# Attention over a gathered half of the tokens: the start in another order, and a batch's mean, its product and its tail rows moved into its own batch

## The reference, cut to what matters

```python
xt = jnp.transpose(x, (0, 2, 1))
q = xt @ Wq.T
qh = q.reshape(B, T, NH, dk).transpose(0, 2, 1, 3)
scores = scale * jnp.einsum('bhqd,bhkd->bhqk', qh, qh)
logits = (scores * cmask + (1.0 - cmask) * NEG) * rmask
attn = jax.nn.softmax(logits, axis=-1)
ctx = jnp.einsum('bhqk,bhkd->bhqd', attn, qh)
out = ctx.transpose(0, 2, 1, 3).reshape(B, T, D) @ Wo.T
return x + jnp.transpose(out, (0, 2, 1))
```

## Time and profile before

| what | value |
|---|---|
| median of 3 runs | 1621.71 us (1619.72 to 1621.74) |
| the profiled execution, its own time | 1617.55 us |
| its span, first to last instruction | 1615.8 us |
| granted TensorE clock, mean | 0.981 |
| busy: TensorE | 1537.4 us (95%) |
| busy: GpSimd | 1339.1 us (83%) |
| busy: VectorE | 1185.3 us (73%) |
| busy: ScalarE | 854.3 us (53%) |

### The profile page before, as it was taken

How to read it: one execution, slowest core, us unless ns; L and a number is a source line. 1 busy time by engine, 2 the same in 40 slices (tenths; PEclk the granted TensorE clock), 3 DMA queues, 4 the chain that set the end, 5 groups by cost and what they waited for, 6 DMA issues and landing times. The chain is left out here.

```text
span 1615.8 us, 33177 instructions
## 1 busy us (share of the span) xinstructions
PE 1537.4 (95%) x10956; PEld 1222.4 (76%) x10956; DVE 1185.3 (73%) x2659; ACT 854.3 (53%) x2055; POOL 1339.1 (83%) x1069
## 2 busy tenths in 40 slices
PE   6798999999999999999999999999999999999995
PEld 3666777787877788787777777777877777777863
DVE  5356787877778787787878778787877778787773
ACT  2145556565555556555555655555555565555450
POOL 5558989898898989889898988989898898987771
PEclk9689999999999999999999999999999999999997
DMA  3434455454544545353554535445554544453410
GB/s 115 107 85 96 105 129 122 110 130 99 129 103 123 122 110 136 93 135 97 123 122 114 136 93 132 100 120 122 123 128 98 129 106 119 115 131 90 109 50 30
DMA packets 93810, 179.09 MB, mean 111 GB/s; under 512 B 24704, under 2 KB 24832, under 8 KB 93632
## 3 DMA queue, kind: packets, MB, share of 16 engines
q1 hardware_dynamic: 64448, 109.71, 30.0%
q0 software_dynamic: 29184, 67.17, 14.9%
HBM read 36.77 MB, written 33.55 MB: 44 GB/s over the span
## 5 line engine op out<-in xcount | busy, mean ns | idle before, releaser
L870 DVE TENSOR_REDUCE small_mxp<-max_scores 108x1 f32<-108x270 f32 x1280 | 546.7, 435 | 269.9 <-PE max_scores L1069 245.4
L751 ACT ACTIVATE small_Pt<-scores,small_kbias 108x270 f32<-108x270 f32 x1280 | 551.5, 483 | 343.9 <-PE scores L1088 335.9
L596 POOL TENSOR_TENSOR small_Pacc<-small_Pacc,small_Pt 108x540 f32<-108x540 f32 x384 | 517.8, 1349 | 117.1 <-ACT small_Pt L751 110.3
L1069 PE MATMUL max_scores<-small_ops 128*108 128x270 f32 x1280 | 412.0, 329 | 17.3 <-DVE small_mxp L870 16.3
L1100 PE MATMUL ctx_psum<-small_Pt,small_V 108*64 108x270 f32 x2560 | 313.1, 391 | 0.0
L900 DVE RECIPROCAL small_rsum<-small_rsum 128x67 f32<-128x67 f32 (+1 forms) x512 | 240.8, 532 | 77.6 <-ACT small_rsum L698 75.8
L1069 PEld LDWEIGHTS max_scores<-small_ops 128*108 128x108 f32 x1280 | 218.9, 173 | 86.3 <-issue 41.0
L1085 PE MATMUL scores<-small_ops 128*108 128x270 f32 x1280 | 270.8, 290 | 4.7 <-ACT small_Pt L751 4.5
L1100 PEld LDWEIGHTS ctx_psum<-small_Pt,small_V 108*64 108x64 f32 x2560 | 184.3, 137 | 106.9 <-issue 0.2
L1088 PE MATMUL scores<-small_ops 128*108 128x270 f32 x1280 | 263.6, 287 | 0.0
L1085 PEld LDWEIGHTS scores<-small_ops 128*108 128x108 f32 x1280 | 191.5, 173 | 25.5 <-ACT small_Pt L751 8.8
(11 more groups left out here) (108 smaller groups left out, 2366.2 us busy)
## 6 DMA issues: line engine op xcount, KB each, us to landing
small_ops<-small_H SPq DMA_DIRECT2D x512, 135.0 KB, 2.8
small_ops<-small_L SPq DMA_DIRECT2D x256, 135.0 KB, 2.7
small_ops<-small_mrow SPq DMA_DIRECT2D x128, 2.1 KB
small_xg<-x_rows,small_idx POOLq DMA_INDIRECT x80, 3.9
small_xtail<-x_rows,small_idx POOLq DMA_INDIRECT x80, 4.9
out_rows<-small_xtail,small_idx POOLq DMA_INDIRECT x80, 3.8
out_rows<-small_xg,small_idx POOLq DMA_INDIRECT x80, 3.8
wq_sb<-wq SPq DMA_DIRECT2D x1, 1024.0 KB, 5.3
```

Source lines behind the costliest of these rows:

```text
L596: nc.gpsimd.tensor_tensor(acc, other, t["Pt"][:R, p0], ALU.add).then_inc(pacc_step, 1)
L751: nc.scalar.activation(t["Pt"][:R, (NT * s + k) % f.NP, half, :], ST[(2 * (NT * h + k) + half) % 3][:R, 0:H], ACT.Exp, bias=t["kbias"][:R, ...
L870: nc.vector.tensor_reduce(t["mxp"][:R, h % 2, m // 2, m % 2:m % 2 + 1], MX[m % 2][:R, 0:H], AX.X, ALU.max).then_inc(mx_red, 1)
L1069: nc.tensor.matmul(MX[m % 2][:R, 0:H], ops[:, OPA, tile_cols(m // 2)], ops[:, OPB, half_cols(m % 2)], start=True, stop=True).then_inc(mx_r ...
```

## The change

It does four things, for the forms that are split (the one that runs here among them).

1. **Front, tables.** Batch 0's one-hots are made alone; those of all batches (`hot_tiles`) after the last xT, and the eight `hot_rows` in pairs behind the first four projections. TensorE makes the other 15 orders, unrolled and with fixed columns, two behind each row-maximum product of head 0 from the third on.
2. **Front, weights.** The transposed Wq is loaded first. GpSimd clears the operands before the gathers, gathers only five tiles of batch 0, and makes one low part. The high and low parts of Wo are made in quarters inside batch 0. G's four blocks are made ahead of the transposes, among them, and (two) among head 1's row-maximum products. VectorE no longer sums.
3. **Loop.** `sum_tokens`, `xbar` and `w` of a batch are made in the batch itself, for the last one too; `w` has one buffer. `xbar` moves from (6, 2) to (5, 2), `w` from (7, 3) and (7, 4) to (5, 3) and (5, 4); pair 5's projections, pair 4's values and pair 6's first projection move later.
4. **Loop, GpSimd.** The tail is gathered in head 0, and its rows are finished and scattered in heads 6 and 7; the 34 jobs are dealt out anew.

The buffers of the one-hot tables and of Wo's parts lie elsewhere in memory. The core of the diff:

```diff
-    ((4, 3), (4, 3), "proj", (4, 0)), ((4, 4), (4, 4), "proj", (4, 1)), ((5, 3), (5, 4), "proj", (5, 0)),
-    ((6, 0), (6, 1), "proj", (5, 1)), ((7, 0), (7, 1), "proj", (6, 0)), ((7, 3), (7, 4), "w", 0)]
-V_STEPS = {1: ((0, 2, 1), (0, 3, 0)), 2: ((4, 0, 0), (4, 0, 1)), 3: ((5, 0, 0), (5, 1, 0)), 4: ((6, 3, 0), (6, 4, 0))}
+    ((4, 3), (4, 3), "proj", (4, 0)), ((4, 4), (4, 4), "proj", (4, 1)), ((5, 3), (5, 4), "w", 0),
+    ((6, 0), (6, 1), "proj", (5, 0)), ((6, 3), (6, 4), "proj", (5, 1)), ((7, 3), (7, 3), "proj", (6, 0))]
+V_STEPS = {1: ((0, 2, 1), (0, 3, 0)), 2: ((4, 0, 0), (4, 0, 1)), 3: ((5, 0, 0), (5, 1, 0)), 4: ((7, 0, 0), (7, 1, 0))}
-XBAR_STEP = (6, 2, 1)
+XBAR_STEP = (5, 2, 1)
-ADD_W_AT = [(0, 0), (0, 1), (0, 3), (0, 4), (1, 0)]
-SCATTER_TAIL_AT = [(1, 1), (1, 3), (1, 4), (2, 0), (2, 1)]
-GATHER_TAIL_AT = [(2, 3), (2, 4), (3, 0), (3, 1), (3, 3)]
-SCATTER_AT = [(3, 4), (4, 0), (4, 1), (5, 0), (5, 1)]
-TAIL_SUM_AT = [(4, 3), (4, 4), (5, 2), (5, 3), (5, 4)]
-GATHER_AT = [(6, 0), (6, 1), (6, 3), (6, 4), (7, 0)]
-SUM_AT = [(7, 1), (7, 2), (7, 3), (7, 4)]
-FIRST_SUM_AT = [(2, 1), (2, 2), (3, 1), (3, 2)]
+WO_HIGH_AT = [(0, 3), (0, 4), (1, 0), (1, 1)]
+WO_LOW_AT = [(1, 3), (1, 4), (2, 0), (2, 1)]
+GATHER_TAIL_AT = [(0, 1), (0, 2), (0, 3), (0, 4), (1, 0)]
+SUM_AT = [(0, 0), (1, 1), (1, 2), (1, 3), (1, 4), (2, 0), (3, 0), (3, 2), (4, 0)]
+SCATTER_AT = [(2, 1), (2, 4), (3, 1), (3, 4), (4, 1)]
+GATHER_AT = [(4, 3), (4, 4), (5, 0), (5, 1), (5, 3)]
+ADD_W_AT = [(6, 0), (6, 1), (6, 3), (7, 0), (7, 2)]
+SCATTER_TAIL_AT = [(6, 2), (6, 4), (7, 1), (7, 3), (7, 4)]
...
-            if (has_prev if name == "out" else has_next if name == "w" or arg[0] >= PAIRS else True):
+            if (has_prev if name == "out" else name == "w" or arg[0] < PAIRS or has_next):
-            whole(XBAR_STEP[2], "xbar", 0, XBAR_STEP[:2])
+        whole(XBAR_STEP[2], "xbar", 0, XBAR_STEP[:2])
...
+            table[GATHER_TAIL_AT[i]].append(("gather", 0, NT + i))
             table[ADD_W_AT[i]].append(("add_w", i))
             table[SCATTER_TAIL_AT[i]].append(("scatter", NT + i))
-            if has_next:
-                table[GATHER_TAIL_AT[i]].append(("gather", 1, NT + i))
-        for i in range(1, NT):
-            if has_third:
-                table[SUM_AT[i - 1]].append(("sum_tokens", 2, i))
-            if not has_prev:
-                table[FIRST_SUM_AT[i - 1]].append(("sum_tokens", 1, i))
+        for i in range(1, form.NTALL):
+            table[SUM_AT[i - 1]].append(("sum_tokens", 0, i))
+        if not has_prev:
+            for i, at in enumerate(WO_LOW_AT):
+                table[at].append(("wo_low", i))
...
-            + [("proj", (2, 0), 0), ("mT", 0, 0), ("xbar", 0, -1), ("w", 0, -1)])
+            + [("proj", (2, 0), 0), ("mT", 0, 0)])
...
-            for dst, src in ((wq_sb, wq), (woT_sb, woT), (wqT_sb, wqT)):
-                sp.dma_start(dst[:], src.rearrange("(k p) n -> p k n", p=P)).then_inc(loaded, 16)
+            for dst, src, landed in ((wqT_sb, wqT, wqT_loaded), (wq_sb, wq, loaded), (woT_sb, woT, loaded)):
+                sp.dma_start(dst[:], src.rearrange("(k p) n -> p k n", p=P)).then_inc(landed, 16)
...
-                    gather(0, k)
+                def clear_operands():
+                    nc.gpsimd.memset(t["ops"][DK:P, :, OPX, :].bitcast(F32), 0.0).then_inc(ops_cleared, 1)
+                    nc.gpsimd.memset(t["ops"][DK:P, :, OPY, :].bitcast(F32), 0.0).then_inc(ops_cleared, 1)
+                    pool.wait_ge(ops_cleared, 2)
+                    nc.gpsimd.memset(t["ops"][DK:DK + 1, :, OPY, :].bitcast(F32), 1.0).then_inc(ops_cleared, 1)
                 if f.split:
-                    for i, (w, name) in enumerate(((wqT_sb, "wqT"), (woT_sb, "woT"))):
-                        pool.wait_ge(whi_done, i + 1)
-                        nc.gpsimd.tensor_tensor(t[name + "_lo"][:], w[:], t[name + "_hi"][:].bitcast(F32),
-                                                ALU.subtract).then_inc(wlo_done, 1)
-                pool.wait_ge(idx_made, 2)
-                if f.split:
-                    pool.wait_ge(wlo_done, 2)
-                nc.gpsimd.memset(t["ops"][DK:P, :, OPX, :].bitcast(F32), 0.0).then_inc(ops_cleared, 1)
-                nc.gpsimd.memset(t["ops"][DK:P, :, OPY, :].bitcast(F32), 0.0).then_inc(ops_cleared, 1)
-                pool.wait_ge(ops_cleared, 2)
-                nc.gpsimd.memset(t["ops"][DK:DK + 1, :, OPY, :].bitcast(F32), 1.0).then_inc(ops_cleared, 1)
-                if f.split:
+                    pool.wait_ge(iotas_made, 5)
+                    clear_operands()
+                    pool.wait_ge(idx_made, 1)
+                    for k in range(NT):
+                        gather(0, k)
+                    pool.wait_ge(ops_cleared, 3)
+                    pool.wait_ge(whi_done, 1)
+                    nc.gpsimd.tensor_tensor(t["wqT_lo"][:], wqT_sb[:], t["wqT_hi"][:].bitcast(F32),
+                                            ALU.subtract).then_inc(wlo_done, 1)
+                    pool.wait_ge(idx_made, 2)
                     for k in range(NT):
                         gather(1, k)
...
+                def keep_G(k, bank):
+                    act.wait_ge(g_made, k + 1)
+                    nc.scalar.copy(G[:, k, :], bank[:, 0:D]).then_inc(g_kept, 1)
+                def wo_high(c):
+                    if c == 0:
+                        act.wait_ge(loaded, 32)
+                        act.wait_ge(idx_made, 2)
+                    nc.scalar.copy(t["woT_hi"][:, c], woT_sb[:, c]).then_inc(whi_done, 1)
                 if f.split:
-                    act.wait_ge(loaded, 48)
+                    act.wait_ge(wqT_loaded, 16)
                     nc.scalar.copy(t["wqT_hi"][:], wqT_sb[:]).then_inc(whi_done, 1)
-                    nc.scalar.copy(t["woT_hi"][:], woT_sb[:]).then_inc(whi_done, 1)
-                for k in range(KD):
-                    act.wait_ge(g_made, k + 1)
-                    nc.scalar.copy(G[:, k, :], MB[k % 2][:, 0:D]).then_inc(g_kept, 1)
...
+                    if b == 0 and pair == 0:
+                        act.wait_ge(wlo_done, 1 + KD)
...
+                if f.split:
+                    keep_G(0, MX[0])
+                    if f.split and (name, arg) == ("xT", NT - 1):
+                        keep_G(1, MX[1])
+                if f.split:
+                    keep_G(2, CT)
+                    keep_G(3, ST[0])
+                    act.wait_ge(idx_made, 2)
...
+                            if f.split and not has_prev and (h, k) in WO_HIGH_AT:
+                                wo_high(WO_HIGH_AT.index((h, k)))
...
+                def first_hot_tiles():
+                    shape = [P, TT, NTALL]
+                    nc.vector.tensor_tensor(t["hot_tile_f"][:, :, 0], t["tileno"][:].unsqueeze(1).to_broadcast(shape),
+                                            t["jh"][:, :, 0].unsqueeze(2).to_broadcast(shape), ALU.is_equal).then_inc(place_step, 1)
+                    dve.wait_ge(place_step, NTALL + 4)
+                    nc.vector.tensor_tensor(t["hot_tile"][:, :, 0], t["hot_tile_f"][:, :, 0],
+                                            tokid[:, :, 0].unsqueeze(2).to_broadcast(shape), ALU.mult).then_inc(onehots_made, 1)
+                def hot_rows(tt):
+                    nc.vector.tensor_tensor(t["hot_row"][:, tt, 1:], t["rowno"][:].unsqueeze(1).to_broadcast([P, B - 1, R]),
+                                            t["jl"][:, tt, 1:].unsqueeze(2).to_broadcast([P, B - 1, R]),
+                                            ALU.is_equal).then_inc(onehots_made, 1)
+                def other_idx():
+                    dve.wait_ge(perm_made, B)
+                    nc.vector.tensor_tensor(t["idx"][:R, 1:],
+                                            ST[2][:R, NTALL:B * NTALL].rearrange("p (b i) -> p b i", b=B - 1),
+                                            t["boff"][:R, 1:], ALU.add).then_inc(idx_made, 1)
+                dve.wait_ge(place_step, NTALL + 3)
+                if f.split:
+                    first_hot_tiles()
+                else:
+                    hot_tiles()
...
-                for tt in range(TT):
-                    nc.vector.tensor_tensor(t["hot_row"][:, tt, 1:], t["rowno"][:].unsqueeze(1).to_broadcast([P, B - 1, R]),
-                                            t["jl"][:, tt, 1:].unsqueeze(2).to_broadcast([P, B - 1, R]),
-                                            ALU.is_equal).then_inc(onehots_made, 1)
-                    if tt == 0:
-                        dve.wait_ge(perm_made, 1)
-                        nc.vector.tensor_tensor(t["idx"][:R, 0], ST[0][:R, 0:NTALL], t["boff"][:R, 0],
-                                                ALU.add).then_inc(idx_made, 1)
+                dve.wait_ge(perm_made, 1)
+                nc.vector.tensor_tensor(t["idx"][:R, 0], ST[0][:R, 0:NTALL], t["boff"][:R, 0],
+                                        ALU.add).then_inc(idx_made, 1)
...
-                dve.wait_ge(perm_made, B)
```

(70 more changed lines are left out.)

133 lines of the change are left out of this document (77 added, 56 removed).

## The result

The median went from 1621.41 us to 1728.1 us (four runs each): a ratio of 1.0655, 95% interval 1.064 to 1.067. The forecast was 1626.0 us in a range of 1611 to 1640. The sign was right, though not for the forecast's reason, as the next lines show; the size was wrong by 102 us, and the time lies far outside the range. The profiled execution has a span of 1726.6 us against 1615.8.

A forecast was written before the change was run, and what follows sets the result against it. The prediction took TensorE, busy for 95% of the span, as the bound, with GpSimd close behind. Front -16, loop +11 and end +9 gave +4 us: a median of 1626 us, range 1611 to 1640.

The forecast's parts named there:

- The front: Everything up to w's old place after G's copies: 94.65 becomes 78.7, -16 us, bounds -22 and -9.
- Rival B: First gather on GpSimd is slow for its own sake and stays 12.3 us longer before the first projection: 1638; chance 0.07.
- clears beside VectorE's two-operand work: In the front, GpSimd's three clears ahead of the first gather: assumed to cost nothing, at most all 4 us.
- GpSimd against that: Loop: five GpSimd jobs in each of heads 6, 7, 0 and 1; TensorE waits 0.6 us at head 0, plus 0.1.
- Rival C: The hold-ups between GpSimd and VectorE add up: 1.5 us a batch and 2 in the end, 1638; chance 0.18.
- The rest of the loop: TensorE's distances and GpSimd's queue in the middle batches: +0.8 us a batch, bounds 0 and +1.5, +11 us over 14.
- L4 to L5: From head 4's row sum to head 5's, in step (6, 2): gains xbar and w, loses a projection; +3.1 us.
- L5 to L6: From head 5's row sum to head 6's: loses xbar and a 0.63 us wait, from 11.12 to 9.6 us.
- L6 to L7: From head 6's row sum to head 7's: gives w for a projection, 11.82 to 9.9 us, perhaps 0.4 wait for VectorE.
- L7 to L0: From head 7's row sum to the next head 0's: stays 10.94 us by TensorE alone, before any wait for GpSimd.
- The end: Last batch now gets xbar, w and sums: +4.6 us and +4.5 us, together +9, bounds 6 and 12.
- Rival A: GpSimd keeps pace in the loop: a batch changes by nothing, the end costs 6.5 us, 1612; chance 0.27.

The follow-up runs named there:

- experiment 1: Against the kernel after: five of GpSimd's nine row sums a batch moved away from the output tiles to middle steps of heads 1 to 4; 1631.59 us, ratio 1.0078.

## Why the prediction was wrong

**The front: right.** Forecast -16 us, measured -18.5 at the first exponential (-16.6 in experiment 1). The first projection came at 30.18 for 29.5, the first reduction at 50.70 for 51.4, two orders between two maxima took 1.44 to 1.61 us, 0.7 to 0.8 each, where 13 / 15 = 0.87 was taken. Rival B fell with the first gather's 1.17 us. One term was mis-sized: "No row shows clears beside VectorE's two-operand work: from nothing (I take this) to all 4 us of it". The clears held VectorE up by 3.4 us (without them idx came at 14.38, with them at 17.81), and it was casts and a `tensor_scalar` that they held, not the two-operand work: eight `scalar_tensor_tensor` with both operands in SBUF, six of them beside the third clear (12.26 to 14.15), took 2.58 us in all, and 2.58 us where no clear ran. Most of it came back: from the end of the fifth gather to the first projection it took 5.5 us (24.67 to 30.18) where 8.4 was forecast, and the orders were faster.

**The step that failed** is the loop's, "GpSimd against that". It charged the new slots on GpSimd's side alone: how long its queue gets, and "where ctx_low (0.7 us) holds GpSimd up as in rows 5, up to 0.4 more, of which I take 0.1". It never asked for the same meeting from VectorE's side, which of VectorE's instructions would now run beside a sum and what stands behind them. `finish_tile`'s second half does, three times a batch, and the reductions that TensorE waits for stand behind it. This is 92.0 us more of that instruction. Moving five sums took 86.2 of them away, and 97.2 us of span with them, 70.5 of TensorE's idle time and 26.7 of its busy time. Rival C named the contention, with the parties reversed and at 0.7 us a batch above the forecast; the batches came out 7.0 above it (101.54 against 94.54).

The trace held the warning: the same instruction spread from 750 to 1942 ns before. In the slots among the output tiles stood scatters and gathers, and only the partial sums could meet it. The change put two-operand sums there.

**The rest of the loop: right within its bounds.** With the sums out of the way (experiment 1) batches are 95.03 us apart by head 7's row sum, +1.3 against a forecast of +0.8, in bounds of 0 and +1.5. Head by head, L4 to L5 takes 13.2 (forecast 9.9 + 3.1 = 13.0), L5 to L6 9.9 (9.6), L6 to L7 10.7 (9.9, with the low part's wait 10.3), L7 to L0 11.4 (10.9 and GpSimd's wait). The wait for GpSimd in head 1 came as the prediction said, 0.4 us in 13 of batches 1 to 14, less than the 0.6 + 0.1 of the sum; so more of the +1.3 than forecast lies on the way from L6 to L7. **The end** was forecast at +9: the last batch is 90.4 instead of 80.9, +9.5, and from L5 to L7 20.6 us for 20.3, with the wait for GpSimd that the prediction named ("some 4 us at the end"):

```profile
1593.21 0.68 PE L1264 MATMUL misc<-small_Pacc,ones 108*64 108x270 f32 x4 [4.43 <-POOL small_Pacc L611]
```

That kernel's 1631.6 us lies 5.6 above the forecast and inside the range. But the kernel before took 1619.3 beside it, so the change without the collision costs 12.3 us where +4 was forecast: some -16.6 for the front (-16), +2 for batch 0 (0), 14 x 1.27 = +18 for the loop (+11) and +9.5 for the end (+9). Every term is inside its bounds or within 2 us, and the small sum of large terms is three times too small. Rival A, GpSimd keeping pace, would have given 1612; even with the sums cut short the time was 1619.4. The range failed because its upper end, 1640, came from the cases of a late GpSimd and a slow first gather, and no case had VectorE late. Three sums of the prediction are off by 0.1 to 0.4 us (31.4 + 0.1 is 31.5, not 31.6; 21.7 - 2.2 + 0.7 is 20.2, not 20.3; 66.2 + 11.5 + 0.6 is 78.3, not 78.7), which decides nothing.

The section of the Trainium skill that the prediction weighed (SBUF — State Buffer, "Who interferes with whom") also holds the rule that decided the case: a VectorE instruction with two SBUF inputs contends with a GpSimd instruction that reads SBUF, and one with at most one such input, outside the two-port modes, doesn't. The trace agrees on both halves (L1008 up to 4408 ns, L1004 at most 753). The prediction used the section for the first gather alone. Its other rule, which it calls inferred, that descriptor generation and a `tensor_tensor` use different sides of the shared ports, the runs don't bear out: in the kernel with the front alone four gathers beside VectorE's one-hot rows took 1.22 to 1.89 us, and the one before those rows 1.01. Which port or lock is behind a hold no run here shows; what is shown is who holds whom, and for how long.

## What to carry to other kernels

Before moving work on GpSimd, list VectorE's instructions whose operands both lie in SBUF and look at the spread, not the mean, of their times: a long maximum is the sign, and what GpSimd ran beside it names what holds them. Price a slot by what runs beside it on the other engine and what is queued behind that, as well as by the room in its own queue; and as the queues shift against each other, read where they meet in the trace and not in the table of slots. Here one row sum right behind a scatter cost a 0.75 us instruction 1.9 us, a row of additions without a gap 3.3 us, and what followed on TensorE could cost more, because its granted clock fell behind the wait in eight of 14 batches.
